# A vision tower on one core: first LayerNorm moved into the second head, three-part expert scores, masked keys in the weight ring, six unused matmuls ahead of QKV

## The reference, cut to what matters

```python
h = concat([cls_tok, h])                          # (32, 65, 64)
h = h + attn(layernorm(h))                        # 8 heads of 8, keys within 32 tokens
x = layernorm(h)
logits = x @ gate_w.T; top, idx = top_k(logits, 6); s = softmax(top)
ffn = x + (sum_k s_k * x @ lattice[idx_k]) @ out_w.T + out_b
h = h + layernorm(ffn) * ln_g + ln_b
```

## Time and profile before

| | us |
|---|---|
| time, median of 3 runs | 1254.29 |
| lowest and highest | 1248.22, 1260.06 |
| profiled execution: its own time | 1258.07 |
| profiled execution: span of the trace | 1256.2 |
| PE busy, mean granted clock | 1124.3 (90%), 0.933 |
| DVE busy | 641.5 (51%) |
| ACT busy | 406.2 (32%) |
| POOL busy | 114.0 (9%) |

### The profile page before, as it was taken

The page is one execution under the profiler, slowest core; times in us unless marked ns, Lnnn a source line. Parts: engine busy times, 40 slices in busy tenths (PEclk is TensorE's granted clock), DMA queues, the critical chain, the costliest instruction groups (busy, mean ns, idle before and its releaser), DMA issues.

```text
span 1256.2 us, 34589 instructions
## 1 busy us (share of the span) xinstructions
PE 1124.3 (90%) x15996; PEld 743.5 (59%) x15996; DVE 641.5 (51%) x872; ACT 406.2 (32%) x554; POOL 114.0 (9%) x108
## 2 busy tenths in 40 slices
...
GB/s 169 103 55 2 83 76 2 22 120 19 2 91 134 4 10 112 44 2 91 68 2 52 106 3 7 99 2 5 55 1 0 2 2 2 1 1 1 6 5 9
DMA packets 24614, 49.26 MB, mean 39 GB/s; under 512 B 9805, under 2 KB 10856, under 8 KB 23829
## 3 DMA queue, kind: packets, MB, share of 16 engines
...
q0 software_dynamic: 432, 0.29, 0.1%
...
## 4 chain that ended last, share of the span: by engine, by line
PE 76%; DVE 12%; DMA 4%; ACT 3%; issue 2%; SPq 1%; POOL 1%; POOLq 0%; ACTq 0%; DVEq 0%
PE PSALL L1103 21%; PE PSALL L961 8%; PE PSALL L1071 7%; PE PSALL L978 6%; PE PSALL L450 5%; DVE WORK L1295 4%; PE PSALL L1094 4%; PE PSALL L1181 4%; PE PSALL L1046 3%; PE PSALL L439 3%; PE PSALL L375 3%; PE PSALL L1191 2%; PE PSALL L440 2%; DMA spec_scr<-MIXED 2%; DVE WORK L1314 1%
## 5 line engine op out<-in xcount | busy, mean ns | idle before, releaser
L1314 DVE STREAM_TRANSPOSE WORK<-PSALL 128x1024 f32<-128x1024 f32 x128 | 152.4, 1229 | 340.2 <-PE PSALL L1071 340.2
L1103 PEld LDWEIGHTS PSALL<-EW,WORK 64*128 64x128 f32 x4096 | 256.4, 197 | 65.1 <-issue 48.7
L1103 PE MATMUL PSALL<-EW,WORK 64*128 64x128 f32 x4096 | 272.7, 288 | 12.4 <-DVE WORK L1314 12.4
L1231 ACT ACTIVATE X<-PSALL,TABLES 128x1024 f32<-128x1024 f32 x128 | 141.7, 1114 | 356.6 <-PE PSALL L1103 356.6
L1295 DVE STREAM_TRANSPOSE WORK<-PSALL 128x1024 f32<-128x1024 f32 x100 | 119.1, 1230 | 58.5 <-PE PSALL L961 54.7
L978 PE MATMUL PSALL<-TABLES,WORK 128*128 128x128 f32 x1000 | 136.4, 284 | 5.0 <-DVE WORK L1295 0.6
L978 PEld LDWEIGHTS PSALL<-TABLES,WORK 128*128 128x128 f32 x1000 | 118.7, 191 | 32.2 <-issue 18.3
L961 PE MATMUL PSALL<-WORK,DW 32*64 32x256 f32 x3200 | 103.3, 389 | 12.6 <-DMA B<-in_fc_b 12.6
L1291 DVE STREAM_TRANSPOSE WORK<-X 128x1024 f32<-128x1024 f32 x96 | 111.4, 1203 | 0.0
L1212 ACT COPY SPEC<-PSALL 128x400 f32<-128x400 f32 x64 | 53.4, 844 | 175.7 <-PE PSALL L978 172.5
L844 DVE TENSOR_TENSOR WORK<-PSALL,X 128x416 f32<-128x416 f32 x160 | 86.6, 584 | 36.5 <-PE PSALL L440 36.4
...
## 6 DMA issues: line engine op xcount, KB each, us to landing
SW<-in_spec_w SPq DMA_DIRECT2D x160, 80.0 KB, 2.4
...
```

The costliest lines, as they stand in the source:

```text
L1103: m = pe.matmul(PS[2 * p + z][:, 2 * b * GRID:(2 * b + 2) * GRID], G[64 * z:64 * z + 64, n % 2, b, h:h + 4, :, c].rearrange("p q o -> p (q ...
L1231: nc.scalar.activation(X[:, n].rearrange("p b (z d) c w -> p d z b (c w)", z=2)[:, p, :, :, 2 * t * GRID:2 * (t + 1) * GRID], PSALL[:, 2 * ...
L1314: nc.vector.transpose(G[:, n % 2, 2 * x + y].rearrange("p h o v -> p o h v"), PSALL[:, 4 + 2 * x:6 + 2 * x, :].rearrange("p k (h o v) -> p ...
```

## The change

The kernel does the same mathematics.

- First LayerNorm: SP issues the loads of `H` during the second head (16 images before the stores of group 1, 12 before those of group 3, the last 4 after all stores as before). DVE centres quarters 0, 1 and 2 and takes the variances of 0 and 1 between its bias additions of images 9 to 15 (`in_head`), and no longer waits for the last stores. The rest of quarter 3 is put among the evacuations of `V`.
- `KMZ` lies in the weight ring; its lower rows and those of `PTZ` are zeroed by POOL as soon as the last mix is done. The eight masked keys of the first chunk are written by ACT during chunks 4 to 7 of QKV. The bias is added to `H` by POOL in four parts during attention.
- `WQKV` gets 64 zero rows below, and the Q and K matmuls use all 128 rows and 128 columns; half of each result is not read. Six matmuls of 128x128x512 that nothing reads run ahead of the tail's first transposes; the ten ahead of the scores are gone.
- Expert scores are written three times, in halves of 32 experts (g = 0, 1), so that each half has 96 rows: high, middle, low. Each tile then needs one spreading matmul. The transposes, high parts and rests double in number (half g has PSUM bank 6 + g to itself), ACT makes the middle part and a copy for the low part in four operations per chunk, POOL subtracts for the low part twice per chunk. `SEL` is written in 12 parts and a zeroing.

The diff, cut; the DVE part is indented anew because its functions now stand in `tail`, and only its new lines are shown.

```diff
-SELECTED = EXPERTS // 8
+SELECTED = EXPERTS // 16
...
-KMZ = modes_mem[:, 0:2 * HEADS * CT].rearrange("p (r h t) -> p r h t", r=2, h=HEADS)
+sw_mem = SW[:].rearrange("p a b c -> p (a b c)")
+KMZ = sw_mem[:, 8320:8320 + 2 * HEADS * CT].rearrange("p (r h t) -> p r h t", r=2, h=HEADS)
...
-SC2 = T1[0:TOK].rearrange("p s a b -> p (s a b)")[:, 0:2 * NIMG * EXPERTS].rearrange("p (b t e) -> p b t e", b=NIMG, t=2)
+SC3 = work[0:TOK, 0:NIMG * 6 * EH].rearrange("p (b g t e) -> p g b t e", b=NIMG, g=2, t=3)
...
+PARTS3 = [sw_mem[:, g * NT // 2:(g + 1) * NT // 2].bitcast(BF16) for g in range(2)]
+REST = [sw_mem[:, at:at + NT] for at in (6 * HT + 1024, 6 * HT + 1024 + NT)]
...
-        x = YT[0:GRID, c * CT:(c + 1) * CT]
+        x = YT[:, c * CT:(c + 1) * CT]
         if c:
             pe.wait_ge(q_ready, c)
-        pe.matmul(PS[2][0:GRID, 0:CT], WQKV[:, 0:GRID], x, start=True, stop=True).then_inc(q_full, 1)
+        pe.matmul(PS[2][:, 0:CT], WQKVZ[:, 0:2 * GRID], x, start=True, stop=True).then_inc(q_full, 1)
         if c:
             pe.wait_ge(k_ready, c)
-        pe.matmul(PS[3][0:GRID, 0:CT], WQKV[:, GRID:2 * GRID], x, start=True, stop=True).then_inc(k_full, 1)
+        pe.matmul(PS[3][:, 0:CT], WQKVZ[:, GRID:3 * GRID], x, start=True, stop=True).then_inc(k_full, 1)
...
+    for i in range(6):
+        pe.matmul(PS[7], ident[:], TABLES[:, :, 0:128], start=True, stop=True)
...
-            for i in range(10):
-                pe.matmul(SPR[0][:, 0, :], ident[:], KMZ[:, 0, 0:4, 0:TOK], start=True, stop=True)
...
-        pe.wait_ge(sc_ready, c + 1)
-        if c >= 2:
-            pe.wait_ge(rest_ready, c - 1)
-        transposes(c, lambda b: SC2[:, b].rearrange("p t e -> p (t e)"), 2 * EXPERTS, PS[6 + c % 2], st_full)
+        for g in range(2):
+            pe.wait_ge(sc_ready, 2 * (c // 2) + g + 1)
+            if c:
+                pe.wait_ge(rest_ready, 2 * c - 1 + g)
+            transposes(c, lambda b: SC3[:, g, b].rearrange("p t e -> p (t e)"), 3 * EH, PS[6 + g], st_full)
...
-            pe.wait_ge(mid_ready, chunks)
-            pe.wait_ge(lo_ready, chunks)
+            pe.wait_ge(lo_ready, 2 * -(-(z + 1) * ZT // CT))
         if n >= 4:
             pe.wait_ge(zx_ready, n - 3)
-        pe.matmul(PS[n % 4][:, 0:ZT], SEL[:, ep, :], SHM[:, z * ZT:(z + 1) * ZT], start=True, stop=False)
-        pe.matmul(PS[n % 4][:, 0:ZT], SEL[:, ep, :], SLOZ[:, z * ZT:(z + 1) * ZT],
-                  start=False, stop=True).then_inc(bc_full, 1)
+        pe.matmul(PS[n % 4][:, 0:ZT], SEL[:, ep % (EH // 2), :], PARTS3[2 * ep // EH][:, z * ZT:(z + 1) * ZT],
+                  start=True, stop=True).then_inc(bc_full, 1)
...
-    act.wait_ge(ho_out.sem, (PASSES * NG - 1) * ho_out.stride // NG)
-    act.dma_start(H[0:1], cls_rows).then_inc(h_in, 16)
-    act.dma_start(H[1:TOK, 0:NIMG - B4], hidden_tokens[:, 0:NIMG - B4]).then_inc(h_in, 16)
...
+    for k in range(LK - 1):
+        deviation(0, k)
     feature_rows(0, GRID, 0)
-    for k in range(2, LK):
-        deviation(0, k)
     for c in range(NC):
+        if c == 3:
+            deviation(0, LK - 1)
+            act.wait_ge(k_ready, 1)
+        if c >= 4:
+            mask_keys(0, range(2 * (c - 4), 2 * (c - 3)))
...
-    mask_keys(0, range(HEADS))
...
+        for g in range(2):
+            act.wait_ge(st_full, 2 * c + g + 1)
+            nc.scalar.copy(PARTS3[g][0:3 * EH, c * CT:(c + 1) * CT], PS[6 + g][0:3 * EH, 0:CT]).then_inc(high_ready, 1)
+    def middle_part(c):
+        for g in range(2):
+            act.wait_ge(rest_ready, 2 * c + g + 1)
+            for r in (EH, 2 * EH):
+                m = nc.scalar.copy(PARTS3[g][r:r + EH, c * CT:(c + 1) * CT], REST[g][r:r + EH, c * CT:(c + 1) * CT])
+            m.then_inc(mid_ready, 1)
+        high_part(c)
+        if c == 2:
+            exp_logits(LK - 1)
+        if c:
+            middle_part(c - 1)
+    middle_part(NC - 1)
...
+    pool.wait_ge(mix_full.sem, PASSES * LAYERS * mix_full.stride)
+    nc.gpsimd.memset(KMZ[GRID:128], 0.0).then_inc(keys_zeroed, 1)
+    pool.wait_ge(keys_zeroed, 1)
+    nc.gpsimd.memset(PTZ[GRID:128], 0.0).then_inc(probs_zeroed, 1)
+    pool.wait_ge(probs_zeroed, 1)
...
+    def residual_and_bias(k):
+        a = slice(k * LB, (k + 1) * LB)
+        nc.gpsimd.tensor_tensor(H[:, a], H[:, a], BP[:].unsqueeze(1).broadcast_to([TOK, LB, GRID]), ALU.add).then_inc(hb_ready, 1)
...
+        if i == 3 * SELECTED:
+            pool.wait_ge(sub_ready, i + 1)
+            nc.gpsimd.memset(SEL[3 * EH:128], 0.0).then_inc(sel_ready, 1)
+            pool.wait_ge(sel_ready, i + 1)
+        if i < NIMG and i % LB == 5:
+            residual_and_bias(i // LB)
...
-    nc.gpsimd.memset(SLOZ[EXPERTS:128], 0.0).then_inc(zeros_set, 1)
-    pool.wait_ge(zeros_set, 1)
+    for g in range(2):
+        nc.gpsimd.memset(PARTS3[g][3 * EH:128], 0.0).then_inc(zeros_set, 1)
+        pool.wait_ge(zeros_set, g + 1)
     for c in range(NC):
         t = slice(c * CT, (c + 1) * CT)
-        pool.wait_ge(lo_copied, c + 1)
-        nc.gpsimd.tensor_tensor(SLO[:, t], REST[0:EXPERTS, t], SLO[:, t], ALU.subtract).then_inc(lo_ready, 1)
+        for g in range(2):
+            pool.wait_ge(mid_ready, 2 * c + g + 1)
+            low = PARTS3[g][2 * EH:3 * EH, t]
+            nc.gpsimd.tensor_tensor(low, REST[g][2 * EH:3 * EH, t], low, ALU.subtract).then_inc(lo_ready, 1)
...
-    nc.vector.memset(KMZ[GRID:128], 0.0).then_inc(keys_zeroed, 1)
-    nc.vector.memset(PTZ[GRID:128], 0.0).then_inc(probs_zeroed, 1)
...
+    def first_norm(k):
+        a = deviations(0, k)
+        nc.vector.tensor_tensor(Y[:, a, 0, :], TMP[:, a], over(st[:, 3, a]), ALU.mult).then_inc(y_ready, 1)
+    def in_head(m):
+        if m in (9, 10):
+            if m == 9:
+                dve.wait_ge(fc1_full.sem, fc1_full.stride + GIMG)
+                dve.wait_ge(h_in, 32)
+            centre(H, m - 9)
+        if m in (11, 12):
+            variances(Y[:, :, 1, :], 0, m - 11)
+        if m == 15:
+            dve.wait_ge(middle_h_in, 16)
+            centre(H, 2)
+    def tail():
+        dve.wait_ge(tail_w, 16 * TAIL_LOADS)
+        variances(Y[:, :, 1, :], 0, 2)
+        for k in range(LK - 1):
+            first_norm(k)
+        nc.vector.memset(V[:, :, :, HD:VH], 1.0).then_inc(ones_set, 1)
+        for c in range(NC):
+            heads = lambda x: x.rearrange("p b (h e) -> p b h e", h=HEADS)
+            if c == 2:
+                dve.wait_ge(last_h_in, 16)
+                centre(H, LK - 1)
+                variances(Y[:, :, 1, :], 0, LK - 1)
+            if c == 4:
+                first_norm(LK - 1)
...
+                thrice = [TOK, LB, 3, EH]
+                nc.vector.tensor_tensor(SC3[:, g, a], SC[:, a, g * EH:(g + 1) * EH].unsqueeze(2).broadcast_to(thrice),
+                                        st[:, 3, a].unsqueeze(2).unsqueeze(3).broadcast_to(thrice), ALU.mult).then_inc(sc_ready, 1)
...
+        def rest(k):
+            for c in range(k * LB // BC, (k + 1) * LB // BC):
+                t = slice(c * CT, (c + 1) * CT)
+                for g in range(2):
+                    dve.wait_ge(high_ready, 2 * c + g + 1)
+                    nc.vector.tensor_tensor(REST[g][0:3 * EH, t], PS[6 + g][0:3 * EH, 0:CT], PARTS3[g][0:3 * EH, t], ALU.subtract
+                                            ).then_inc(rest_ready, 1)
...
+            if p == PASSES - 1 and n == 1:
+                sp.wait_ge(ho_out.sem, ho_out.stride)
+                sp.dma_start(H[0:1], cls_rows).then_inc(h_in, 16)
+                sp.dma_start(H[1:TOK, 0:GIMG], hidden_tokens[:, 0:GIMG]).then_inc(h_in, 16)
+            if p == PASSES - 1 and n == NG - 1:
+                sp.wait_ge(ho_out.sem, ho_out.stride + 128 * n)
+                sp.dma_start(H[1:TOK, GIMG:NIMG - B4], hidden_tokens[:, GIMG:NIMG - B4]).then_inc(middle_h_in, 16)
             passes.wait(fc2_ready, B4 * (n + 1))
...
+            if p == PASSES - 1:
+                in_head(m)
...
-        passes.wait(ho_out, NG)
+        if p + 1 < PASSES:
+            passes.wait(ho_out, NG)
...
+    nc.gpsimd.memset(WQKVZ[GRID:128], 0.0).then_inc(wide_zeroed, 1)
+    pool.wait_ge(wide_zeroed, 1)
```

More of the change, by code:

```diff
@@ L513, in tail_scalar @@
             act.wait_ge(k_ready, NC)
-            def mask_keys(c, heads):
-                for h in heads:
-                    nc.scalar.activation(KM[:, c % 2, h, :], KT[:, c * CT:(c + 1) * CT], ACT.Copy,
-                                         scale=HM[:, h:h + 1]).then_inc(km_ready, 1)
-            mask_keys(0, range(HEADS))
             for i in range(LN_STEP + LK * LB):
@@ L681, in centre, with variances @@
                 nc.vector.tensor_tensor(TMP[:, a], src[:, a], over(st[:, 0, a]), ALU.subtract).then_inc(centred, 1)
[L683 removed]
+            def variances(squares, n, k):
                 a = slice(k * LB, (k + 1) * LB)
@@ L691, in deviations @@
                 return a
-            dve.wait_ge(tail_w, 16 * TAIL_LOADS)
-            dve.wait_ge(h_in, 32)
-            for k in range(LK + 1):
```

(52 more changed lines are left out.)

283 lines of the change are left out of this document (152 added, 131 removed).

## The result

The changed kernel takes 1194.8 us in the median of four runs (1191.2 to 1197.2), the kernel before 1255.1 in four runs beside it (1248.2 to 1260.1). The ratio is 0.952 with a 95% interval of 0.947 to 0.957; the prediction was 1193, in 1181 to 1214. The profiled execution took 1191.2 us, with a span of 1189.3.

A forecast was written before the change was run, and what follows sets the result against it. PE was taken to bound the expert loop and QKV (at half clock), DVE routing. Terms -20.8 - 13.8 - 11.1 + 0 + 8 - 24 = -61.7 took 1258.1 to 1196.4 us profiled, 1193 median; range 1181 to 1214.

The forecast's parts named there:

- LayerNorm in the head: From the head's end to the second chunk's V: LayerNorm work moved between bias additions, -20.8 us (-22 to -16).
- The 2 us that it adds if the clock still falls: Ahead of QKV: 2 us more if the clock falls in PE's 1.8 us gap before the six unused matmuls.
- The added 0.95 for the delayed addition: End of the head: image 15's bias addition waits behind the third centring, starting about 895.4 instead of 894.45.
- QKV: Second chunk's V to last copy: 2.4 us per chunk instead of 4.47, if the clock is full, -13.8 us.
- Rival A: QKV stays at 1.2 GHz and attention starts cold, about +3 us there; 1211 us in all, chance 0.18.
- The busy-time rule: QKV: clock follows how busy PE has lately been, so wider tiles buy nothing; same 1211 us as Rival A.
- Masks and unused matmuls: QKV's last copy to the first score: scores follow at once, without masked keys and ten matmuls there, -11.1 us.
- Attention: Attention: POOL loses selector casts, gains a zeroing and four bias parts; 0 us (-1 to +4).
- Routing: Routing: wider score writing, more rests, waits on single banks and a slower end, +8 us (+5 to +10).
- Experts: Expert loop: two spreading matmuls less per step, -28.0 us, less PE's waits for DVE; -24 us (-28 to -19).
- the 1 us that I credited to the start: Start of the expert loop: fewer matmuls before the first product win 1 us.

The follow-up runs named there:

- e5: The changed kernel with each spreading matmul of the expert loop issued twice: 1217.7 us in four runs, ratio to the kernel before 0.969.
- e8: The changed kernel with the third LayerNorm's projections, centring and finish further apart in the expert loop: 1201.5 us.
- e6: The changed kernel with DVE's centrings and variances of quarters 0 to 2 back behind the head's last bias addition: 1209.4 us.
- e10: The changed kernel with DVE's centrings and variances behind the head's last bias addition and nine unused matmuls instead of six: 1197.3 us.
- e2: The changed kernel without the six unused matmuls ahead of QKV, Q and K kept wide: 1207.6 us.
- e4: The changed kernel with Q and K of 128 rows but only 64 columns of weights: 1194.2 us.
- e1: The changed kernel with Q and K of 64 rows and 64 columns again, the six unused matmuls kept: 1203.3 us.
- e3: The changed kernel with Q and K of 64 rows and 64 columns and without the six unused matmuls: 1205.9 us.
- e11: The changed kernel with the first chunk's eight masked keys written after QKV instead of during chunks 4 to 7: 1195.7 us.
- e7: The changed kernel with ACT's middle and low copies of chunks 4 to 7 put after the last high part: 1198.5 us.
- e12: The changed kernel with the edits of e9, e7 and e8 together: 1189.8 us in six runs, ratio to the kernel before 0.947.
- e9: The changed kernel with three unused matmuls ahead of QKV instead of six: 1186.0 us.

## Why the prediction was right, and where its reasons were not

**LayerNorm in the head (-20.8 with the addition's delay; measured -21.7).** The terms held: the addition was put behind the third centring, the loads of `H` didn't hold it, and the six matmuls took 5.3 us to the first transposes, as forecast, and set the start. (Scaled from the 0.465 us that the prediction names, six would take 5.5.) The 2 us that it adds if the clock still falls came in e5 and e8, as 1.7. The added 0.95 for the delayed addition measured 0.2. But the reason for the size was incomplete. e6 and e10 show that the move in time is worth 4.6 us with the clock held. The rest is then what left this place (the scaling of 4.47 us beside POOL's addition, the zeroing of 3.5 us, the late bank) and the full clock of the first chunk; these were not tried one by one. The move also shortens PE's wait behind the six, so that the clock is still up when QKV starts. That dependence, worth 15.5 us, was not in my sum.

**QKV (-13.8; measured -13.4).** The chunk of 2.4 us was 2.35. That the clock would be full came true, but my reason for it fell, so this term was right by luck: I argued from the share of time in which the whole array is filled, as in attention. e2 has that mix and stays at 0.50 for all of QKV; e4 has half the columns and holds 1.00. What the runs show in its place: with 128 rows in Q and K a clock that is up stays up, and it must be up when QKV starts. Rival A would have come with either of the two edits missing: QKV is then 12.8 (e2) or 13.4 us (e1) longer. The busy-time rule of the Trainium skill ("TensorE: Matmul & The Clock Gate", "What's actually happening") fits the fall in e2 and e6, where PE was idle for 4 us. It doesn't fit e1, where the clock fell in a stretch with PE at 100%, nor the 35 us of e2 and e3 in which PE was busy in 34.9 and 34.8 at 0.50.

**Masks and unused matmuls (-11.1; measured -10.7).** Right: e11 gives 3.2 for the masks, which cost nothing where they are now.

**Attention (0; measured -0.7).** Right, and the -0.7 is within what the clock does there. With one dip to 0.50 of 3.4 us at 8 to 13 us behind the first score (before, e4, e7, e12) attention takes 94.3 to 94.5 us, with a dip of 6.8 us (e5, e8, e10) 95.2 to 95.3, with none (e9) 92.8, and the changed kernel, whose dip stands at the start, 93.5. Rival A's 3 us for a cold start of attention were wrong: e1, e2 and e3 start it at 0.50 and take 93.8 us, 1 us more than e9.

**Routing (+8; measured +7.3).** The sum is right, two terms in it aren't. Score writing went from 1.62 to 2.16 for the pair in three quarters, and from 1.82 to 2.36 in the last, so +2.2 where I had 3.1. In the last chunks a chunk takes 2.5 and 2.4 us, not 1.9: I took 0.36 for one of ACT's copies, they are 0.41, and they were in the loop's way in full, since ACT also makes both high parts. From the last score writing (1057.6) to the first tile are 7.1 us, 3.6 before: +3.5, where I had +3.4 to the first spreading.

**Experts (-24; measured -22.8).** The step of 1.31 was exact, the 160 matmuls are all of the gain (e5), and PE waits in three places as foreseen, but for 0.9 us each instead of 1.5: +2.6 (3.0 with the short waits ahead of them) where I had 4 to 5. What failed is the 1 us that I credited to the start. What is left of the stage beside steps and waits was 137.7 - 80 x 1.66 = 4.9 us, and is now 114.9 - 80 x 1.31 - 2.6 = 7.5: a loss of 2.6. The half clock alone is not the reason: both loops start at 0.50 (chain steps of 2.6 and 2.3 us at 1065.40 and 1068.01 in the changed kernel), and before it came up in this stretch:

```profile
1112.00:1113.00 1.00, 1.00 (x6) 0.21 (x3) 0.12 (x1) 0.00 (x0) 1.00 (x1) 0.85 0.06 16
```

That is 5.0 us into the stage as the table bounds it, with PE busy in all of them; after the change it is 6.8 us, of which PE waits 0.65 for DVE's first multiplication, which stands behind the last subtraction. Half of the busy time at half clock is lost: 2.5 before, 3.1 after. So 0.6 of the 2.6 us are the clock's, 0.65 that wait and 0.4 the three short waits; I estimate these from the traces, and the remaining 1 us is open. e7's edit, which takes that wait away, gave 0.8 back.
